# A two-layer transformer block on one core: the two batches' linear-attention, feature and context stages woven in another order

## The reference, cut to what matters

```python
# LayerNorm runs ahead of every block
x = x + L0_attn(ln(x))    # linear attention: q, k = elu(.) + 1; out = q.cumsum(k v) / q.cumsum(k); projection Wo
x = x + L0_xattn(ln(x))   # features exp(z), exp(-z) of x and of a context of 77 rows; softmax over the 77; projection fc
x = x + L0_ffn(ln(x))     # "spline": cluster gates, argmax, one-hot table lookup, LayerNorm at its end
x = x + L1_attn(ln(x))    # causal softmax attention, 16 heads of 16
x = x + L1_xattn(ln(x), ctx, mask)
x = x + L1_ffn(ln(x))     # 16 experts, the best 4 of each token, and a shared one
```

## Time and profile before

| what | value |
|---|---|
| median of three runs | 1293.87 us (1292.87 to 1296.69) |
| the profiled execution: its own time | 1288.8 us |
| its span, first to last instruction | 1287.5 us |
| mean granted TensorE clock | 0.917 |
| busy: PE, DVE, ACT, POOL | 84%, 66%, 43%, 30% of the span |
| the chain that ended last | PE 50%, DVE 26%, issue 8%, ACT 7% |

### The profile page before, as it was taken

One profiled execution on the slowest core, in us unless ns is written; L12 is line 12 of the kernel. 1 busy time (PEld: TensorE's weight loads), 2 busy tenths in 40 slices (PEclk: granted clock), 3 DMA queues, 4 the chain that ended last, 5 costly groups with the idle time before them and its releaser, 6 DMA issues.

```text
span 1287.5 us, 19411 instructions
## 1 busy us (share of the span) xinstructions
PE 1079.4 (84%) x6344; PEld 655.7 (51%) x6344; DVE 844.3 (66%) x2302; ACT 552.6 (43%) x1128; POOL 385.1 (30%) x430
## 2 busy tenths in 40 slices
PE   4688878987768985788899998999896888989994
PEld 2244644665434563324344444435555457877873
DVE  4777648668468758587677677726766964733476
ACT  2333036521245652354656644675452442434431
POOL 3331023320146421013200011002421740677772
PEclk9998988995779996588999999999996998998997
DMA  6246639552000360303233302006000220554665
GB/s 197 72 100 131 90 52 318 147 91 30 1 0 25 98 112 0 50 1 62 84 53 51 50 10 42 2 2 183 26 1 1 89 72 19 160 183 148 199 198 201
DMA packets 63201, 107.90 MB, mean 84 GB/s; under 512 B 13433, under 2 KB 35291, under 8 KB 62816
## 3 DMA queue, kind: packets, MB, share of 16 engines
q1 hardware_dynamic: 55104, 76.61, 26.5%
q0 software_dynamic: 7680, 17.07, 3.6%
q10 hardware_dynamic: 320, 12.98, 3.0%
HBM read 74.75 MB, written 48.89 MB: 96 GB/s over the span
## 4 chain that ended last, share of the span: by engine, by line
PE 50%; DVE 26%; issue 8%; ACT 7%; POOL 4%; DMA 3%; SPq 1%; ACTq 0%; POOLq 0%; DVEq 0%
PE psum L1047 5%; PE psum L926 5%; PE psum L712 4%; DVE mx L1793 4%; PE psum L896 4%; PE psum L948 4%; PE psum L824 3%; PE psum L799 3%; POOL rows_by_slot L2142 2%; DVE H L1380 2%; PE psum L1066 2%; DVE small L1557 2%; PE psum L810 2%; PE psum L611 2%; DVE work L1570 2%
## 5 line engine op out<-in xcount | busy, mean ns | idle before, releaser
L1793 DVE TENSOR_REDUCE mx<-psum 128x1 f32<-128x512 f32 (+3 forms) x384 | 195.9, 551 | 80.4 <-PE psum L896 40.8
L896 PE MATMUL psum<-stack_area 96*128 96x512 bf16 (+3 forms) x288 | 99.2, 355 | 30.5 <-DVE mx L1793 26.6
L1289 ACT ACTIVATE work<-psum 128x512 f32<-128x512 f32 (+1 forms) x192 | 92.4, 527 | 58.2 <-PE psum L951 38.1
L799 PE MATMUL psum<-area 128*128 128x308 f32 x256 | 101.6, 484 | 16.5 <-DVE area L1527 8.5
L2084 POOL TENSOR_TENSOR work<-work,small 128x308 f32<-128x308 f32 x108 | 75.8, 708 | 121.4 <-DVE small L1573 121.2
L2003 POOL TENSOR_SCALAR rstd<-mv 128x4 f32<-128x4 f32 (+1 forms) x26 | 6.1, 236 | 333.6 <-DVE mv L1390 279.4
L948 PE MATMUL psum<-stack_area 98*128 98x512 bf16 (+3 forms) x288 | 95.1, 343 | 12.5 <-ACT work L1289 5.9
L1289 ACT ACTIVATE HT<-psum 128x384 f32<-128x384 f32 (+2 forms) x192 | 80.8, 466 | 52.6 <-PE psum L951 36.0
L1047 PE MATMUL psum<-area,work 128*128 x384 | 94.5, 391 | 5.7 <-ACT work L1321 5.7
L810 PE MATMUL psum<-const_tile,work 128*77 128x128 f32 x512 | 79.7, 281 | 12.7 <-ACT stack_area L1210 8.9
L810 PEld LDWEIGHTS psum<-const_tile,work 128*77 128x77 f32 x512 | 62.2, 151 | 49.3 <-POOL work L2084 28.3
(11 more groups left out here) (266 smaller groups left out, 2452.1 us busy)
## 6 DMA issues: line engine op xcount, KB each, us to landing
rows_by_slot<-in_unused_rows ACTq DMA_DIRECT2D x2, 6336.0 KB, 31.3
W<-rows_by_slot SPq DMA_DIRECT2D x48, 264.0 KB, 2.8
stack_area<-parts_a0q SPq DMA_DIRECT2D x24, 128.0 KB, 4.2
stack_area<-parts_a0k SPq DMA_DIRECT2D x24, 128.0 KB, 6.7
stack_area<-parts_a1q SPq DMA_DIRECT2D x24, 128.0 KB, 4.5
stack_area<-parts_a1k SPq DMA_DIRECT2D x24, 128.0 KB, 6.5
H<-outs_by_token SPq DMA_DIRECT2D x6, 512.0 KB, 4.1
area<-outs_by_token SPq DMA_DIRECT2D x6, 512.0 KB, 6.2
```

The source lines that it names most:

```text
L799: done = pe.matmul(s, queries[:, g // 2 if masked else g, t * P:(t + 1) * P], keys[:, g, :, :].rearrange("p j k -> p (j k)"), start=True, ...
L896: done = pe.matmul(u.bank(k)[:, 0:cols], stack["q"][0:KSTACK, j, t * P:(t + 1) * P], stack["k"][0:KSTACK, j, half * SPAN:half * SPAN + col ...
L1289: act.activation(p[:, 0:cols], u.bank(k)[:, 0:cols], ACT.Exp).then_inc(*u.empties(k))
L1793: dve.tensor_reduce(mxt[n % 2][:, j, t, half:half + 1], u.bank(k)[:, 0:cols], AX.X, ALU.max).then_inc(*u.empties(k))
```

## The change

On every engine the order becomes:

1. `linear_heads(0)` beside the rest of `linear_inputs(1)`, which now takes five steps for four and is drained.
2. `linear_heads(1)` beside `attention_out(0)` and `feature_inputs(0)`, which begin two steps later.
3. `context(0)` beside `attention_out(1)`.
4. `feature_inputs(1)` and `context(1)` (58 steps) beside the chain of batch 0, three steps of it for two, so 87 of its 99; the last 12 are drained alone.
5. Eight steps of the chain of batch 1 (its four projections and four steps of its LayerNorm) run ahead of the first maximum.

`linear_heads` becomes one loop over 32 items with no break between groups and a lag of three steps instead of two; a half group's copy, transposes and division follow at fixed distances, in the stream of the next group. The slots of the stacks of batch 1 alternate from slot 0, and its first stack is loaded in the last group of batch 0, without the wait for the first context. In its place ACT's first copies of `context(0)` wait until batch 1's scores are made, and DVE's context waits until batch 1's sums and transposes are. The rows of -1 are filled in twelve copies of 2 by 1024, eight in `linear_heads(0)` and four in the first steps of `context(0)`. The values of the context pass through `work[6 + b]` instead of `work[0]`. The PSUM banks of projection and features move to other pairs.

```diff
+FEATURES_LEAD = 2
+EARLY_STEPS = 8
...
-HEADS_LAG = 2
+HEADS_LAG = 3
...
-        STACK_SLOTS = (0, 1, 0, 1, 1, 0, 1, 0, 1, 0, 2, 1, 0, 2, 1, 0)
+        STACK_SLOTS = (0, 1, 0, 1, 0, 1, 0, 1, 1, 0, 2, 1, 0, 2, 1, 0)
...
+        plan_heads(0, MAIN_T)
+        plan_heads(1, SIDE)
+        plan_out(0, MAIN_T)
+        plan_features(0, MAIN_T)
+        plan_context(0, "b")
+        plan_out(1, SIDE)
+        plan_features(1, MAIN_T)
+        plan_context(1, "b")
...
+        HEAD_ITEMS = GROUPS * TILES
+        HEADS_STEPS = HEAD_ITEMS + HEADS_LAG + 3
+
+        def last_of_half(item):
+
+            if 0 <= item < HEAD_ITEMS and item % TPS == TPS - 1:
+                return item // TILES, item % TILES // TPS
...
-            advance(e["linear_heads"](0), other)
-            advance(chain(pause(1), e["attention_out"](0, "a"), e["feature_inputs"](0), e["context"](0, "b")), other)
+            advance(e["linear_heads"](0), other, extra_every=4)
+            drain(other)
+            other = chain(e["attention_out"](0, "a"), e["feature_inputs"](0))
+            advance(e["linear_heads"](1), other, FEATURES_LEAD)
+            drain(other)
+            other = e["attention_out"](1, "a")
+            advance(e["context"](0, "b"), other, FEATURES_LEAD)
             drain(other)
             e["between"]("linear")
             other = chain(e["context_out"](0, "b"), e["spline"](0), e["attention_inputs"](0))
-            advance(chain(e["linear_heads"](1), pause(1), e["attention_out"](1, "a"), e["feature_inputs"](1), e["context"](1, "b")), other)
+            advance(chain(e["feature_inputs"](1), e["context"](1, "b")), other, extra_every=2)
             e["between"]("contexts")
             drain(other)
-            e["between"]("softmax")
             side, done = chain(e["context_out"](1, "b"), e["spline"](1), e["attention_inputs"](1)), GROUPS * GROUP_STEPS + WEIGHTED_LEAD + 12
+            advance(pause(EARLY_STEPS), side)
             maxima, weighted = e["maxima"](), e["weighted"]()
...
+                for n in range(HEADS_STEPS):
+                    if n < HEAD_ITEMS:
+                        g, t = n // TILES, n % TILES
+                        slot = slot_of["a", b, g]
+                        stack = stacks[slot]
+                        if t == 0:
+                            pe.wait_ge(stack_landed[slot].sem, 16 * STACK_DMAS * loads_by["a", b, g])
+                        pe.wait_ge(*score.vacant(n))
+                        for j in range(HPG):
+                            done = pe.matmul(score.bank(n)[:, j * P:(j + 1) * P], stack["k"][0:KSTACK, j, t * P:(t + 1) * P],
+                                             stack["q"][0:KSTACK, j, t * P:(t + 1) * P], start=j == 0, stop=True, skip_group_check=True)
+                        done.then_inc(*score.fills(n))
+                    m = n - HEADS_LAG
+                    if 0 <= m < HEAD_ITEMS:
+                        g, t = m // TILES, m % TILES
+                        c, q = t // TPS, t % TPS
+                        bank = heads[c].bank(2 * g)
+                        if q == 0:
+                            pe.wait_ge(*heads[c].vacant(2 * g))
+                        if t:
+                            if g == 0:
+                                pe.wait_ge(*state.empty(t - 1))
+                            pe.matmul(bank[:, q * P:(q + 1) * P], states[b][:, t - 1, g * P:(g + 1) * P], qfeats[b][:, g // 2, t * P:(t + 1) * P],
+                                      start=q == 0, stop=False, skip_group_check=True)
+                        pe.wait_ge(*score.empty(m))
+                        a = work[m % 4]
+                        for j in range(HPG):
+                            done = pe.matmul(bank[j * STRIP:(j + 1) * STRIP, q * P:(q + 1) * P], vaug[b][:, t, g * HPG + j, :],
+                                             a[:, j * P:(j + 1) * P], start=t == 0, stop=True, skip_group_check=True)
+                        done.then_inc(linear_summed, 1)
+                    if last := last_of_half(m - 1):
+                        g, c = last
+                        pe.wait_ge(*heads[c].empty(2 * g))
+                        head_turn(b, heads[c], 2 * g + 1, work[4 + c])
+                    yield
...
-                pe.wait_ge(rows_set, 3)
+                pe.wait_ge(rows_set, 3 * HPG)
...
+                    if b == 0 and n < 2 * HPG:
+                        if n == 0:
+                            act.wait_ge(mask_ready, 1)
+                        minus_ones(n // HPG, n % HPG)
+                    if last := last_of_half(n - HEADS_LAG):
+                        g, c = last
+                        if g:
+                            act.wait_ge(*heads[c].full(2 * g - 1))
+                        elif b:
+                            act.wait_ge(*u_heads["a", 0][c].full(2 * GROUPS - 1))
+                        head_copy(heads[c], 2 * g, work[4 + c], (linear_summed, b * HEAD_ITEMS + n - HEADS_LAG + 1))
+                    yield
...
+                    if (phase, b) == ("b", 0) and n < HPG:
+                        if n == 0:
+                            act.wait_ge(linear_summed, BATCH * HEAD_ITEMS)
+                            for s in range(2):
+                                act.wait_ge(split_stored[1][s].sem, 128)
+                        minus_ones(2, n)
...
+                        elif q == 0 and (phase, b) == ("b", 0):
+                            act.wait_ge(*u_scores["a", 1].full(HEAD_ITEMS - 1))
...
+            def minus_ones(slot, j):
+                act.copy(stacks[slot]["k"][KSTACK:KSTACK + 2, j, :], const("sign")[KSTACK:KSTACK + 2, :].to_broadcast([2, SEQ])).then_inc(rows_set, 1)
...
+                for n in range(HEADS_STEPS):
+                    if n < HEAD_ITEMS:
+                        before = b * HEAD_ITEMS + n - 3
+                        dve.wait_ge(*score.full(n))
+                        if before > 0:
+                            dve.wait_ge(linear_summed, before)
+                        dve.tensor_tensor(work[n % 4][:, :].rearrange("p (j n) -> p j n", j=HPG), score.bank(n).rearrange("p (j n) -> p j n", j=HPG),
+                                          const("causal01").unsqueeze(1).to_broadcast([P, HPG, P]), ALU.mult).then_inc(*score.empties(n))
+                    if last := last_of_half(n - HEADS_LAG - 2):
+                        g, c = last
+                        head_norm(b, g, c, heads[c], 2 * g + 1, DEN_EPS)
+                    yield
...
+                if b:
+                    dve.wait_ge(*u_ctx_turn[phase, 0].full(count - 1))
+                elif masked:
                     dve.wait_ge(weighted_done, 12 * len(GROUP_ORDER))
                 else:
-                    dve.wait_ge(*u_ctx_turn["e", 0].full(count - 1))
+                    dve.wait_ge(linear_summed, BATCH * HEAD_ITEMS)
+                    for heads in u_heads["a", 1]:
+                        dve.wait_ge(*heads.full(2 * GROUPS - 1))
                 for n in range(count + TURN_LAG[phase] + SUMS_LAG):
                     i = n - DIVIDE_LAG
...
-                if (phase, b) == ("a", 1) and slot == 0:
-                    sp.wait_ge(ctx_summed, 8)
...
+                    elif b == 0:
+                        load_stacks("a", 1, 0)
+                    yield from pause(TILES)
+                yield from pause(HEADS_STEPS - HEAD_ITEMS)
 
```

98 lines of the change are left out of this document (11 added, 87 removed).

## The result

The changed kernel takes 1313.78 us (median, 1313.11 to 1316.89, four runs) against 1294.64 us beside it (1292.87 to 1296.69): a ratio of 1.0152, 95% interval 1.0129 to 1.0175. It is slower, by 1.5%; I had forecast 1283.6 us, faster. Its profiled execution took 1313.32 us with a span of 1311.8 us, 24.3 us above the span before.

What follows compares the result with a forecast made beforehand. No engine was taken as full throughout; the change would fill PE's gaps with dense work. Stages from 99 us ended at 461.5 against 478.4, less 6.6 owed: 10.3 us gained, 1293.9 to 1283.6 us, range 1266 to 1303.

Steps and rivals of the forecast that it cites:

- linear_heads(0): First stage, from 99 us: 54.35 us of PE work plus 4 us of idle kept, 58.5 us (55 to 62).
- linear_heads(1): Stage with attention_out(0) and feature_inputs(0): PE bounds it, some 4 us lost at the LayerNorm, 63 us (59 to 67).
- context(0): Stage with attention_out(1): PE work of 57 us, 1 us for ACT's copies, stage 59 us (56 to 62).
- context(1) with 60 chain steps: context(1) beside batch 0's chain: DVE bounds it with 82 us of work, 97 us (89 to 120).
- DVE fills 0.83 to 0.86: Rule for context(1)'s stage: DVE's share from two stretches where it was the bound turns 82 us into 99 or 95.
- Rival B: In context(1)'s stage PE falls to its lower clock and becomes the bound: 120 us, kernel 1306.6 us; chance 0.15.
- Rival C: Nothing measurable: DVE waits on POOL divisions cost 6.4 us, the uncovered drain 4 more, 1294 us; chance with D 0.20.
- no price: For DVE's two-input instructions beside POOL's divisions: no slowdown, from 688 ns with POOL quiet and 692 with it busy.
- A: Dense stages pay more: DVE fills 0.92 in context(1)'s stage, 89 us; 15 us more gained, 1268.6 us; chance 0.19.
- D: Stacks, not PE, pace linear_heads: 12 us in place of 3, kernel 1292.6 us; chance together with Rival C 0.20.
- The drained and early steps: After context(1): 12 drained and eight early steps take 37 us (32 to 43); early steps hide 7 us of stack load.
- The owed maxima: At the common point in the softmax stage, 12 maxima already done before are still to do: 6.6 us.

Runs made afterwards that it cites:

- e4_loop_alone: The kernel before, in its own order of stages, with only the new one-loop linear_heads of lag 3; ratio 0.9969, 1290.4 us.
- The filler: The changed kernel with four or eight extra unread bf16 matmuls ahead of each score of context(1); ratio 1.0103 with four, 1.0131 with eight.
- e5_chain_alone: The changed kernel with feature_inputs(1) and context(1) issued with nothing beside them, then batch 0's chain alone; ratio 1.0137 to the kernel before.
- e2_wx_later: The changed kernel with the loads of w_x and one bias row put behind the drained 12 chain steps; ratio 1.0122 to the kernel before.
- e8_loop_early: e4_loop_alone with the eight early steps of chain 1 ahead of the maxima; ratio 0.9971 to the kernel before.
- e7_both: The changed kernel with the edits of e3_one_for_one and e2_wx_later together; ratio 1.0011 to the kernel before.
- e3_one_for_one: The changed kernel with one chain step, not three for two, per step of feature_inputs(1) and context(1); ratio 1.0056, 1301.2 us.

## Why the prediction was wrong, point by point

**linear_heads(0), forecast 58.5, measured 64.6.** PE's work was right (54.0 us against 54.35). The idle was 10.6 and not 4: the breaks of the closed groups did go, but DVE's copy of a running state of batch 1 (L1474) was late by 3.9 us, ACT's copies of the heads by 2.7 in three waits, DVE's work on batch 1's features (L1446) by 2.1, a stack by 1.4. I had removed stalls without saying what is late next. e4_loop_alone shows the same from the other side: with the one loop, the last transposes of linear_heads(0) end at 162.7, against 162.1 before, no gain.

**linear_heads(1), forecast 63, measured 59.0; context(0), 59 and 57.9.** Right, and the first with too much caution: the clock is 1.00, the LayerNorm stall is filled by heads items.

**feature_inputs(1), 48 and 49.9.** Right.

**context(1) with 60 chain steps, forecast 97, measured 121.1.** This is the step that failed. DVE's work was right: 80.4 us against 82. The engine that I took for the bound was wrong, and so was the rule that turned work into time, "DVE fills 0.83 to 0.86". I had that fill from stretches in which the second stream was linear_heads(1) or the maxima, which have many independent items ready. In the new stage both streams are chains of DVE, ACT, POOL and PE, and DVE's share falls with their density: 0.82, 0.74 and 0.66 where 20, 40 and 60 steps of the chain stand beside it. A sum of an engine's work is a lower bound; what stands above it depends on who else waits in the stream.

**Rival B** had the size (120 us for this stage) and put it down to PE at its lower clock. The clock was low, 0.69 (0.57 from 345 to 385, where PE was busy 34.1 of 40). But it had PE as the bound over 0.92 of the stage, and PE was busy for 0.77. The filler gave 10 us of the 24 back, with its own time taken off and the clock at 0.82, so the clock's part is 10 us or more. The rest I put down to the two streams' waits for each other; no run takes them away at a full clock and this weave, so the split is not measured. B was a part of the cause. I had given it 0.15, since "at the lower clock PE would be busy for nearly all of the stage", which was no reason against it.

**Rival C**: its drain, but not its contention, decided anything. DVE's two-input instructions do run longer beside POOL's work than I had read from the earlier trace rows: L1421 took 811 ns in the changed kernel, and the spline's more. The first line is of the changed kernel, the second of e5_chain_alone, where no division runs beside the chain:

```profile
L1751 DVE SCALAR_TENSOR_TENSOR area<-area 128x128 f32<-128x128 f32 x1 | 0.7, 716 | 0.0
```

```profile
L1751 DVE SCALAR_TENSOR_TENSOR area<-area 128x128 f32<-128x128 f32 x1 | 0.3, 291 | 0.0
```

Over the lines L1421, L1763, L1675, L1746, L1751 and L1777 the difference between the two kernels, for the same number of instructions, is about 3.5 us of DVE's time. But one line goes the other way by 3.0 us, since in e5_chain_alone POOL's additions of the same chain run right beside it (again the changed kernel first, then e5_chain_alone with POOL's line):

```profile
L1780 DVE TENSOR_TENSOR area<-area,bias_row 128x256 f32<-128x256 f32 x8 | 3.4, 425 | 8.8 <-ACT area L1289 8.7
```

```profile
L1780 DVE TENSOR_TENSOR area<-area,bias_row 128x256 f32<-128x256 f32 x8 | 6.0, 794 | 0.8 <-ACT area L1289 0.7
...
432.66 6.86 POOL L2129 TENSOR_TENSOR X<-X,area 128x256 f32<-128x256 f32 x8 [1.37 <-DVE area L1780]
```

"GPSIMD Engine Reference" of the Trainium skill (Specifications) says that GpSimd's SBUF interfaces are shared with VectorE, with contention for DVE instructions with two SBUF inputs; these rows agree. So my "no price" was wrong for the single instruction, and over the chain, woven against alone, about right (0.5 us).

**Rivals A and D.** A had DVE denser than the forecast; it was thinner. D had the stacks as the pace of linear_heads: PE's waits for stacks over both linear_heads are 1.4 and 0.8 us, not 12.

**The drained and early steps, forecast 37, measured 44.4.** The terms were right but for one: behind SP's issues I had looked only at stacks. The load of w_x now meets the chain's last stores; 6.4 us in one wait, shown by e2_wx_later. That the early steps hide the stack's load was right, and my 7 us lie within what the runs give (5 to 10).

**The owed maxima, 6.6 us**, and the rows of -1 at nothing: right, 24.1 of 24.3 us come out.

**The deeper error** is in the first part of the prediction: "takes that work away from beside the long chain of batch 0. Both sides must be priced". I priced the front by idle times that I could see, and the back by the work that goes. linear_heads(1) and attention_out(1) were cheap where they stood. From context(0)'s last sum to context(1)'s the kernel before took 209 us for these two, main and the chain; main and the chain by themselves, one after the other, take 193.1. So the 32 heads items (30.7 us of PE in my sum) and the projection cost 16 us there, and 32.4 in their new place. Rows that could have said so were in front of me: a chain with PE busy for 27.43, 22.51 and 16.24 us in stretches of 34, 24 and 30.5 is one that needs a partner with ready work. "Perfetto Trace Analysis" of the Trainium skill (Optimization Strategy) says that a kernel with several regimes may gain from interleaving them. Here that holds for the weave with the heads, and at one for two and one for one with the context (10 to 15 us); at three for two it hardly holds, 191.0 without the stall against 193.1.

**What stays open.** The waits that DVE and PE hand each other were read from the timeline and their growth from the doses; they were not taken away by themselves, with more score banks or a longer lag, since the kernel's plan has all eight PSUM banks in use. So that the waits make the rest of the loss is argued from the doses, not shown alone. Why the second 20 chain steps cost 1.55 us each and the first 0.56 is not separated into density and the part of the chain that they bring. The best version found is e4_loop_alone, 0.3% below the kernel before; its interval ends at 0.9992, and e8_loop_early is as good.

## What to carry to other kernels

Before independent work is moved out from beside a long dependent chain, run or estimate the two alone: if the chain alone is long and its engines take turns, what stands beside it is cheap, and moving it away buys little. Two latency-bound streams woven in order can take nearly as long as one after the other; the fill of an engine with an independent partner can't be carried over to a dependent one. And when a chain's end moves, look at what every queue issues at the old place: a bulk load can meet small stores that the chain waits for.

## What the runs showed of the hardware that I had not expected

With a 1 MB load issued ahead of it, a 128 KB store of the changed kernel landed 7.5 us after its issue, where others took 1.7. TensorE's granted clock was 0.57 from 345 to 385 us of the changed kernel, near the lower of its two levels (1.2 GHz), while PE was busy for 34.12 of 40 us with 96 float32 matmuls; in the next part, with 59 in 11.25 of 17 us, it was 1.00. Four small bf16 matmuls ahead of each score lifted the mean over the stage from 0.69 to 0.82, eight to 0.93. PE's busy time over the stage went from 93.2 to 83.9 us with four, 15 us of filler in it, so the same work from 93.2 to 69.

On the chips where the kernel before took 1359 us the extra time lies behind 1000 us: from there e7_both takes 361.0 us and e3_one_for_one, on one of the faster chips, 299.8, with nearly the same number of instructions and PE busy for 263.4 and 257.2 of it. It stands in idle time for which the profile names no engine ("issue") or only a "remote" one. One line of the two, e3_one_for_one first:

```profile
L1066 PE MATMUL psum<-area,work 128*128 x384 | 94.0, 389 | 5.7 <-ACT work L1353 5.7
```

```profile
L1066 PE MATMUL psum<-area,work 128*128 x384 | 95.4, 393 | 15.8 <-issue 15.8
```

What the engines wait for there, the profile doesn't show, and no run was made to find it.
